# 16-wide attentions: contexts divided through DMA and VectorE instead of transposes, and one score unit moved behind the value products

## The chip, the cores and the metric

One core of a Trainium2 chip runs the whole program in one launch. The metric is the device time of one execution in microseconds. The kernel before took 1924.47 us (median of three runs, 1923.56 to 1924.92).

## The reference

Four layers on an input of 2 x 512 x 512 in float32; each is an attention and a feed-forward block, and both are followed by x = layernorm(x + block(x)). The attentions of layers 0, 2 and 3 have 32 heads of 16 values, and only these three are touched here. Layer 0 has 8 key and value heads, biases and rotary positions; layer 2 has 32 key and value heads and biases; layer 3 has 8 key and value heads, no biases and no rotation. In short:

```python
scores = einsum('bihd,bjhd->bhij', q, k) * SCALE      # d = 16
scores = where(causal, scores, lowest)
attn   = softmax(scores, axis=-1)
out    = einsum('bhij,bjhd->bihd', attn, v)           # heads joined again to 512 values: the context
return out @ wo
```

## The kernel before

The three 16-wide attentions are instances of one class, `Attention16`: a0 (layer 0, with rotation, here called narrow), a2 (layer 2, `wide`, 32 key heads) and a3 (layer 3, narrow, no rotation). Each runs 16 steps, one for a group of four heads: 8 groups for each of the two batches. Every engine has its own list of instructions, in program order; engines wait for one another on counting semaphores only.

A step `s` has ten slots `k` on TensorE (line 686 on). In slot k TensorE computes transposed scores of group s (`scoresT`, L574, into PSUM bank 4 or 5), ScalarE takes their exponential (`exp`, L1023) into the buffer PB, and GpSimd masks it (`causal`, L929). `scoresT` may only start when the exponential two slots earlier is done. So that the exponential stays in range, the maximum of every row is needed first: it comes from a first pass over the scores, two steps ahead. That pass is cut into six units a = 0 to 5 (`scores`, L539 and L541); VectorE takes the maximum of a unit straight after it (`maxima`, L801, L803, L806). Units use two pairs of PSUM banks in turn, so unit u waits until the maximum of unit u-2 is taken. GpSimd splits the maxima of a group into three bfloat16 parts (`split_max`, L913 to L919), TensorE transposes them in slot 3 of the next step (`max_T`, L551), ScalarE copies them (`take_max`, L1013), and the queue of SyncE (SP) writes them as three rows into KQ (`load_max`, L1107). Slot 0 of a step waits for that DMA.

Behind `max_T` in slot 3 stand the value products of the group before (`pv`, L595, 32 matmuls into bank 7). Their output lies transposed: 16 values and the sum of the probabilities for each head. ScalarE copies it to OT behind the exponential of slot 6 (`take_out`, L1040), TensorE turns it back in slot 8 (`back`, four transposes, L605), and VectorE divides by the sums (`norm`: a reciprocal at L815 and a product at L819) into CTX. In slot 1 of every odd step, two groups together are transposed again (`ctx_T`, L613), and ScalarE copies them to XTT (`take_ctx`, L1034), where the output projection reads them (`out_part`, L620).

Other work is spread over the steps. TensorE's part is in `aside`: the projections of the second batch (`project`, L485, and `project_v`, L500), and from step 10 (wide: 11) on the output projection of the first batch and the transposes of its layernorm (`turn_first`, L226). VectorE's part is in `beside(dve, st, s, a)`, called after the maximum of unit a: at a = 2 it does the rotation in a0 (`turn`, L765 to L768, in steps 2, 3, 5, 7, 9), the rounding rest in a3 (`take`, L752, same steps), `take_v` in a2 (L780, steps 1 and 2), and from step 11 (wide: 12) on the layernorm of the first batch (`mean`, L265 to L272, and one step later `finish`, L279). At k = 6 ScalarE's list has `middle` (L1004) in a3 ahead of `take_out`. GpSimd's list has `low` (L903) in a3 behind the mask of slot 8. In steps 2 to 5 and 10 to 13 of a0 and a2 it also has a bias addition (L979) behind slot 9.

SP's list in `sync` goes through groups: `load_max(G)` (done during step G-1), then `load_rows` of a late chunk (six to nine DMAs of the rounded parts into KQ: HI, MID, LOW), then, from G = 12, prefetches of weights. SP waits in this order, too.

These lines fix where the moved unit stands, and what VectorE does right behind it:

```python
if more and k in (0, 1, 2, 5, 6, 7):
    self.scores(pe, s + 2, (0, 1, 2, 5, 6, 7).index(k))
...
for a in range(6):
    if s + 2 < last:
        self.maxima(dve, s + 2, a)
    self.beside(dve, st, s, a)
```

Of the kernel before, what the change touches and what calls it, by code (L numbers as in the profile page):

```python
# [106 lines left out]
def build(nc, d, out):  # L107
# [11 lines left out]
    with ctx:  # L119
# [241 lines left out]
        def variances(dve, st, b):  # L361
# [10 lines left out]
        CTX = sb("CTX", [P, 2, NT, P], F32, A16)  # L372
# [9 lines left out]
        RC = sb("RC", [P, NT, 4], F32, A16)  # L382
        A16.close()
# [5 lines left out]
        AUX = 6  # L389
        s16 = {k: sig("a16_" + k) for k in (  # L390
            "ones_loaded proj_psum v_psum v_ready pads_ready turned rotated hi_ready rest_ready mid_ready lo_ready "
            "rows0_loaded rows1_loaded rows2_loaded scores_ready max_ready max_step max_parts maxT_psum maxT_ready "
            "max0_loaded max1_loaded scoresT_ready exp_ready probs_ready pv_ready outT_ready out_psum ctx_ready "
            "ctxT_psum ctxT_ready biased").split()}

        class Attention16(Stage):
            def __init__(self, W, Wo, nkv, scale, loaded, cols=None, vbias=None, rope=False, bo=None,
# [26 lines left out]
                    outT_ready=16, out_psum=16, ctx_ready=16, ctxT_psum=8, ctxT_ready=8,  # L424
# [175 lines left out]
            def back(self, pe, G):  # L600
# [56 lines left out]
            def tensor(self, pe):  # L657
# [29 lines left out]
                for s in range(last):  # L687
                    more = s + 2 < last
                    for k in range(10):
                        self.scoresT(pe, s, k)  # L690
                        self.aside(pe, s, k)
                        if more and k in (0, 1, 2, 5, 6, 7):
                            self.scores(pe, s + 2, (0, 1, 2, 5, 6, 7).index(k))
                        if k == 1 and s >= 3 and s % 2:
                            self.ctx_T(pe, (s - 3) // 2, 7)
# [5 lines left out]
                        if k == 8 and s:  # L701
                            self.back(pe, s - 1)
# [107 lines left out]
            def norm(self, dve, st, G):  # L810

                on = self.on
                dve.wait_ge(on["out_psum"].sem, on["out_psum"].at(G + 1))
                o = PS[:, 7, :].rearrange("p (t h e) -> p t h e", t=NT, h=4)
                st.link(dve.reciprocal(RC[:, :, :], o[:, :, :, HD]))  # L815
                if G >= 4 and G % 2 == 0:
                    dve.wait_ge(on["ctxT_psum"].sem, on["ctxT_psum"].at(G // 2 - 1))
                c = CTX[:, G // 2 % 2, :, G % 2 * 64:G % 2 * 64 + 64].rearrange("p t (h e) -> p t h e", e=HD)
                dve.tensor_tensor(c, o[:, :, :, 0:HD], RC[:, :, :].unsqueeze(3).to_broadcast([P, NT, 4, HD]),  # L819
                                  ALU.mult).then_inc(s16["ctx_ready"].sem, 1)  # L820

            def vector(self, dve, st):
# [30 lines left out]
                for s in range(last):  # L853
# [4 lines left out]
                    if s:  # L858
# [167 lines left out]
            def take_ctx(self, act, C, bank):  # L1026
# [3 lines left out]
                act.wait_ge(on["ctxT_psum"].sem, on["ctxT_psum"].at(C + 1))  # L1030
                if c == 0:
                    act.wait_ge(on["proj_psum"].sem, on["proj_psum"].at(self.each * (b + 1)))
                    act.wait_ge(on["v_psum"].sem, on["v_psum"].at((b + 1) * (NT if self.wide else 1)))
                act.copy(XTT[:, b, c, :], PS[:, bank, :]).then_inc(s16["ctxT_ready"].sem, 1)  # L1034

            def take_out(self, act, G):

                on = self.on
                act.wait_ge(on["pv_ready"].sem, on["pv_ready"].at(3 * G + 3))
                act.copy(OT[:, :], PS[:, 7, :]).then_inc(s16["outT_ready"].sem, 1)  # L1040

            def scalar(self, act):
# [59 lines left out]
            def load_max(self, sp, G):  # L1102
# [5 lines left out]
                  .then_inc(s16["max%d_loaded" % (G % 2)].sem, 16)  # L1108

# [35 lines left out]
            def sync(self, sp, prefetch):  # L1145
# [12 lines left out]
                for G in range(1, NB * GROUPS):  # L1158
                    self.load_max(sp, G)
# [1707 lines left out]
```

## Time and profile before

| | |
|---|---|
| median of three runs | 1924.47 us |
| profiled execution | 1924.28 us, its span 1922.6 us |
| mean granted TensorE clock | 0.993 of full speed |
| TensorE, VectorE, ScalarE, GpSimd busy | 95, 59, 45, 45% of the span |
| a0, 16 steps | from about 52 to 234 us of the span |
| a2, 16 steps | from about 1333 to 1529 us |
| a3, 16 steps | from about 1632 to 1810 us |

A profile lists instructions with start and length by engine. PE is TensorE's matmuls, PEld its weight loads, DVE VectorE, ACT ScalarE, POOL GpSimd, SPq the DMA issues of SyncE. An arrow in square brackets tells how long the engine stood still and whose work ended the wait. The length of a matmul includes its way through the array, so it is longer than the distance to the next one.

### The profile page before, as it was taken

The numbers are of one execution on the slowest core, as the hardware profiler recorded it, in microseconds if no ns is written. First come the engines' busy times: TensorE is split into PE (matmuls) and PEld (weight loads), VectorE is DVE, ScalarE is ACT, GpSimd is POOL, SyncE is SP. The second block draws the span as 40 slices with busy tenths as digits, with TensorE's granted clock in tenths as the row PEclk, the third lists the DMA queues.
The fourth block names the chain that finished last, engine by engine and source line by source line (L and its number), as shares of the span: only waits on it lengthen the run. The fifth ranks groups of instructions, "written<-read, shape, count | busy, mean of one in ns | idle before, by whom it ended". The sixth has DMA issues, their size and how long they took to land.

```text
span 1922.6 us, 29645 instructions
## 1 busy us (share of the span) xinstructions
PE 1828.2 (95%) x10760; PEld 1287.9 (67%) x10760; DVE 1130.6 (59%) x2433; ACT 859.2 (45%) x1896; POOL 871.5 (45%) x1383
## 2 busy tenths in 40 slices
PE   7999999999999999999999899999999999999998
PEld 3454447888888888888888687764455454555466
DVE  5677467666666666666666424235556355666465
ACT  1566544444444444444444433314466502565441
POOL 2465426555555555555554444323355312444352
PEclk9899999999999999999999999999999999999999
DMA  7213000101010101010100234205123104211101
GB/s 230 55 46 114 2 18 1 55 1 56 1 55 1 56 1 56 1 56 1 56 1 33 83 115 148 88 1 129 52 69 100 47 1 94 54 36 46 53 10 45
DMA packets 47201, 99.28 MB, mean 52 GB/s; under 512 B 8011, under 2 KB 36043, under 8 KB 43595
## 3 DMA queue, kind: packets, MB, share of 16 engines
q1 hardware_dynamic: 44464, 95.02, 15.6%
q10 hardware_dynamic: 2592, 2.36, 0.5%
q8 instruction: 87, 1.43, 0.3%
q14 instruction: 58, 0.48, 0.1%
HBM read 66.36 MB, written 2.10 MB: 36 GB/s over the span
## 4 chain that ended last, share of the span: by engine, by line
PE 76%; DVE 12%; ACT 4%; issue 3%; DMA 1%; POOL 1%; ACTq 1%; PEld 0%; SPq 0%; PEldq 0%; POOLq 0%; DVEq 0%
PE PS L1483 10%; PE PS L1582 9%; PE PS L485 6%; PE PS L2005 5%; PE PS L595 5%; PE PS L574 4%; PE PS L620 4%; PE PS L1560 4%; PE PS L1544 3%; DVE NM L801 3%; PE PS L2018 3%; PE PS L539 3%; PE PS L1512 3%; PE PS L1976 2%; PE PS L500 2%
## 5 line engine op out<-in xcount | busy, mean ns | idle before, releaser
L1023 ACT ACTIVATE PB<-PS 128x512 f32<-128x512 f32 x480 | 276.4, 600 | 213.1 <-PE PS L574 210.3
L929 POOL TENSOR_SCALAR_AFFINE_SELECT PB<-PB 128x256 f32<-128x256 f32 (+1 forms) x480 | 173.7, 369 | 283.6 <-ACT PB L1023 274.6
L801 DVE TENSOR_REDUCE NM<-PS 128x2 f32<-128x1024 f32 x192 | 206.8, 1090 | 147.3 <-PE PS L541 143.8
L574 PE MATMUL PS<-KQ 99*128 99x512 bf16 (+3 forms) x768 | 179.1, 305 | 9.3 <-ACT PB L1023 4.6
L1774 ACT CAST OTH<-PS 128x512 fp32r<-128x512 f32 x64 | 37.6, 587 | 309.5 <-PE PS L1565 309.5
L1901 POOL TENSOR_SCALAR PR<-PR,RCP 128x512 f32<-128x512 f32 (+3 forms) x256 | 135.5, 540 | 83.3 <-DVE RCP L1704 83.3
L1836 ACT ACTIVATE PR<-PR,NX 128x512 f32<-128x512 f32 (+3 forms) x256 | 145.0, 566 | 32.5 <-DVE NX L1698 29.3
L485 PE MATMUL PS<-XTT,WA 128*128 128x512 f32 x288 | 145.9, 613 | 13.5 <-DVE ident_masks_b L2647 12.0
L1698 DVE CUSTOM_DVE_ANT_0 PR<-PS,CAUSAL 128x512 f32<-128x512 f32 (+3 forms) x256 | 124.3, 486 | 53.3 <-PE PS L1531 52.0
L539 PE MATMUL PS<-KQ 99*128 99x128 bf16 (+2 forms) x576 | 125.2, 278 | 22.6 <-DVE NM L801 20.5
L1662 DVE TENSOR_TENSOR PTL<-PS,PTH 128x384 fp32r<-128x384 f32 (+2 forms) x256 | 115.5, 452 | 28.3 <-ACT PTH L1767 25.9
L541 PE MATMUL PS<-KQ 125*128 125x128 bf16 x768 | 126.9, 222 | 1.7 <-DVE NM L803 1.7
L295 POOL TENSOR_TENSOR rstd<-ve,halfneg 128x1 f32<-128x1 f32 x64 | 44.1, 689 | 168.9 <-DVE ve L272 168.9
L1544 PE MATMUL PS<-ident_masks,PR 128*128 128x128 f32 x640 | 111.9, 273 | 8.1 <-DVE PTL L1662 7.9
L574 PEld LDWEIGHTS PS<-KQ 99*128 99x128 bf16 x768 | 62.4, 99 | 78.4 <-issue 39.2
L539 PEld LDWEIGHTS PS<-KQ 99*128 99x128 bf16 x576 | 56.6, 99 | 78.2 <-DVE NM L801 43.7
L1690 DVE TENSOR_TENSOR XBB<-PS,XBB 128x512 f32<-128x512 f32 x64 | 44.3, 692 | 105.2 <-PE PS L1582 104.4
L1767 ACT CAST PTH<-PS 128x384 fp32r<-128x384 f32 (+2 forms) x256 | 101.0, 395 | 8.3 <-PE PS L1544 7.9
L1582 PE MATMUL PS<-Wo1H,OTL 128*128 128x512 f32 x256 | 102.1, 399 | 0.0
L1582 PE MATMUL PS<-Wo1H,OTH 128*128 128x512 f32 x256 | 100.9, 394 | 0.5 <-DVE OTL L1683 0.5
L1582 PE MATMUL PS<-Wo1L,OTH 128*128 128x512 f32 x256 | 100.4, 392 | 0.0
L541 PEld LDWEIGHTS PS<-KQ 125*128 125x128 bf16 x768 | 71.7, 99 | 39.2 <-issue 27.9
(333 smaller groups left out, 4578.4 us busy)
## 6 DMA issues: line engine op xcount, KB each, us to landing
KQ<-HI SPq DMA_DIRECT2D x90, 128.0 KB
KQ<-MID SPq DMA_DIRECT2D x72, 128.0 KB
WB<-f_w SPq DMA_DIRECT2D x12, 768.0 KB, 4.4
WB<-w1o SPq DMA_DIRECT2D x8, 1024.0 KB, 7.9
WC<-f_w SPq DMA_DIRECT2D x10, 768.0 KB, 4.4
WB<-w1a SPq DMA_DIRECT2D x8, 768.0 KB, 4.3
WB<-w1b SPq DMA_DIRECT2D x8, 768.0 KB, 5.8
WA<-w SPq DMA_DIRECT2D x6, 1024.0 KB, 6.4
```

The lines of the kernel that those rows point to most:

```text
L485: x = pe.matmul(PS[:, self.bank(m), :], self.W[:, c, at:at + P], XTT[:, b, c, :], start=(c == 0), stop=(c == NC - 1))
L539: pe.matmul(ps[:, 0:n - P], KQ[0:PR16, self.query(G, h), i * P:(i + 1) * P], KQ[0:PR16, self.key(G, h), 0:n - P], start=True, stop=True)
L541: x = pe.matmul(ps[:, n - P:n], KQ[0:KR, self.query(G, h), i * P:(i + 1) * P], KQ[0:KR, self.key(G, h), n - P:n], start=True, stop=True)
L574: x = pe.matmul(ps[:, at:at + T - j * P], KQ[0:PR16, self.key(s, h), j * P:(j + 1) * P], KQ[0:PR16, self.query(s, h), j * P:T], start=True ...
L801: x = dve.tensor_reduce(nm[:, h:h + 2, i], PS[:, b:b + 2, 0:(i + 1) * P], AX.X, ALU.max, negate=True)
L929: pool.affine_select(blocks, blocks, [[0, count], [1, P]], ALU.is_ge, 0.0, base=0, channel_multiplier=-1).then_inc(s16["probs_ready"].sem, 1)
L1023: act.activation(PB[:, n % PBS, :], PS[:, 4 + n % 2, :], ACT.Exp, scale=self.scale)\
L1483: x = pe.matmul(PS[:, p % 2, :], a[:, c, n:n + P], x[:, c, :], start=(c == 0 and i == 0), stop=(c == NC - 1 and i == 2))
L1544: x = pe.transpose(PS[:, 4 + i % 2, j * P:(j + 1) * P], PR[:, n % 2, OFF[t] + j * P:OFF[t] + (j + 1) * P], ident[:, :])
L1582: x = pe.matmul(PS[:, 6 + t % 2, :], o[:, h, t * P:(t + 1) * P], w[:, h, :], start=(h == 0 and i == 0), stop=(h == GQ - 1 and i == 2))
L1836: act.activation(PR[:, n % 2, at:at + w], PR[:, n % 2, at:at + w], ACT.Exp, scale=-1.0, bias=NX[:, n % 2, i:i + 1], accum_out=SM[:, n % 2, ...
L1901: pool.tensor_scalar(pr, pr, RCP[:, n % 2, i:i + 1], 1.0, ALU.mult, ALU.mult)\
```

## The change

The contexts of groups 0 to 13 no longer go back through TensorE. When OT is written, SP copies the sums of four heads to a tile SUMS spread over 128 partitions, and the 16 undivided rows of each head straight into XTT (`spread`, five DMAs for each group). For every two groups VectorE takes the reciprocal of SUMS (`invert`, behind the maximum of unit 1 in odd steps), SP brings it back into eight rows and from there repeats it over 128 partitions (`gather_inverse`, two DMAs, and `spread_inverse`, one), and in the next even step VectorE multiplies XTT by it in place (`scale_ctx`). The last two groups go the old way. ScalarE's copy in slot 1 goes, and the third score unit stands in slot 4, behind `pv`, instead of slot 2.

```diff
+        TURNED = NB * GROUPS - 2
...
                 elif part == 0:
-                    pe.wait_ge(on["ctx_ready"].sem, on["ctx_ready"].at(G))
-                    if G % 2 == 0:
-                        pe.wait_ge(on["ctxT_ready"].sem, on["ctxT_ready"].at(G // 2))
+                    pe.wait_ge(on["outT_ready"].sem, on["outT_ready"].at(G))
+                    if G > TURNED:
+                        pe.wait_ge(on["normed"].sem, on["normed"].at(TURNED // 2 + G - TURNED))
...
-                        if more and k in (0, 1, 2, 5, 6, 7):
-                            self.scores(pe, s + 2, (0, 1, 2, 5, 6, 7).index(k))
-                        if k == 1 and s >= 3 and s % 2:
-                            self.ctx_T(pe, (s - 3) // 2, 7)
+                        if more and k in (0, 1, 4, 5, 6, 7):
+                            self.scores(pe, s + 2, (0, 1, 4, 5, 6, 7).index(k))
...
-                        if k == 8 and s:
+                        if k == 8 and s > TURNED:
                             self.back(pe, s - 1)
...
+            def invert(self, dve, C):
+                on = self.on
+                dve.wait_ge(on["out_loaded"].sem, on["out_loaded"].at(160 * (C + 1)))
+                dve.reciprocal(SUMS[:, :, :], SUMS[:, :, :]).then_inc(s16["normed"].sem, 1)
+
+            def scale_ctx(self, dve, C):
+                on = self.on
+                b, c = divmod(C, NC)
+                dve.wait_ge(on["inv_loaded"].sem, on["inv_loaded"].at(48 * (C + 1)))
+                dve.tensor_tensor(XTT[:, b, c, :], XTT[:, b, c, :], SPREAD[:, :], ALU.mult)\
+                   .then_inc(s16["ctxT_ready"].sem, 1)
...
-                    if s:
+                    if s > TURNED:
                         self.norm(dve, st, s - 1)
...
+                if a == 1 and s >= 3 and s % 2:
+                    self.invert(dve, (s - 3) // 2)
+                if a == 1 and s >= 4 and s % 2 == 0:
+                    self.scale_ctx(dve, (s - 4) // 2)
+                if a == 5 and s == NB * GROUPS - 1:
+                    self.scale_ctx(dve, TURNED // 2 - 1)
...
                 act.wait_ge(on["pv_ready"].sem, on["pv_ready"].at(3 * G + 3))
+                if 1 <= G <= TURNED:
+                    act.wait_ge(on["out_loaded"].sem, on["out_loaded"].at(80 * G))
...
                         self.exp(act, s, k)
-                        if k == 1 and s >= 3 and s % 2:
-                            self.take_ctx(act, (s - 3) // 2, 7)
...
+            def spread(self, sp, G):
+                on = self.on
+                C, e = divmod(G, 2)
+                b, c = divmod(C, NC)
+                if c == 0 and e == 0:
+                    sp.wait_ge(on["proj_psum"].sem, on["proj_psum"].at(self.each * (b + 1)))
+                    sp.wait_ge(on["v_psum"].sem, on["v_psum"].at((b + 1) * (NT if self.wide else 1)))
+                sp.wait_ge(on["outT_ready"].sem, on["outT_ready"].at(G + 1))
+                loaded = s16["out_loaded"]
+                sp.dma_start(SUMS[:, e, :], OT[HD:P:32, :]).then_inc(loaded.sem, 16)
+                for h in range(4):
+                    a = 64 * e + HD * h
+                    sp.dma_start(XTT[a:a + HD, b, c, :], OT[32 * h:32 * h + HD, :]).then_inc(loaded.sem, 16)
+
+            def gather_inverse(self, sp, C):
+                on = self.on
+                sp.wait_ge(on["normed"].sem, on["normed"].at(C + 1))
+                if C:
+                    sp.wait_ge(on["inv_loaded"].sem, on["inv_loaded"].at(48 * C))
+                for e in range(2):
+                    sp.dma_start(INV[4 * e:4 * e + 4, :], SUMS[:, e, :]).then_inc(s16["inv_loaded"].sem, 16)
+
+            def spread_inverse(self, sp, C):
+                on = self.on
+                sp.wait_ge(on["inv_loaded"].sem, on["inv_loaded"].at(48 * C + 32))
+                if C:
+                    sp.wait_ge(on["ctxT_ready"].sem, on["ctxT_ready"].at(C))
+                sp.dma_start(SPREAD[:, :], INV[:, :].unsqueeze(1).to_broadcast([8, HD, T]))\
+                  .then_inc(s16["inv_loaded"].sem, 16)
...
-                for G in range(1, NB * GROUPS):
-                    self.load_max(sp, G)
+                for G in range(1, NB * GROUPS + 1):
+                    if G >= 4 and G % 2 == 0:
+                        self.gather_inverse(sp, (G - 4) // 2)
+                    if G < NB * GROUPS:
+                        self.load_max(sp, G)
+                    if G >= 4 and G % 2 == 0:
+                        self.spread_inverse(sp, (G - 4) // 2)
+                    if 2 <= G <= TURNED + 1:
+                        self.spread(sp, G - 2)
+                    if G == NB * GROUPS:
+                        break
                     if self.wide and G in (2, 3):
                         self.load_rows(sp, 4 + G)
                     if G - self.lag in self.late:
```

## Rows read from the trace of the kernel before

**Rows 1.** Page: busy time by engine; the chain that ended last, by engine.

```profile
PE 1828.2 (95%) x10760; PEld 1287.9 (67%) x10760; DVE 1130.6 (59%) x2433; ACT 859.2 (45%) x1896; POOL 871.5 (45%) x1383
...
PE 76%; DVE 12%; ACT 4%; issue 3%; DMA 1%; POOL 1%; ACTq 1%; PEld 0%; SPq 0%; PEldq 0%; POOLq 0%; DVEq 0%
```

**Rows 2.** Timeline of PE, a2, step 6: start, length, engine, line, operation.

```profile
1420.82 0.66 PE L605 MATMUL PS<-ident_masks,OT 128*128 128x128 f32 x4
1421.32 0.88 PE L574 MATMUL PS<-KQ 99*128 99x256 bf16 x3
```

**Rows 3.** Timeline, a0, steps 7 to 8.

```profile
137.31 2.36 PE L595 MATMUL PS<-PB,WC 128*32 128x512 f32 x32
...
138.28 0.74 DVE L765 SCALAR_TENSOR_TENSOR WB<-PS,bcols,WB 128x512 f32<-128x512 f32 x1
...
139.60 0.61 PE L574 MATMUL PS<-KQ 99*128 99x384 bf16 x4
...
140.59 1.82 DVE L801 TENSOR_REDUCE NM<-PS 128x2 f32<-128x768 f32 x2
...
143.46 0.33 PE L539 MATMUL PS<-KQ 99*128 99x384 bf16 x1
...
144.17 1.23 DVE L801 TENSOR_REDUCE NM<-PS 128x2 f32<-128x1024 f32 x1
...
145.46 0.34 PE L539 MATMUL PS<-KQ 99*128 99x384 bf16 x1 [0.73 <-DVE NM L801]
...
148.57 0.61 PE L574 MATMUL PS<-KQ 99*128 99x384 bf16 x4
```

**Rows 4.** Groups by line over the whole span: count, busy us, mean ns, idle before.

```profile
L1023 ACT ACTIVATE PB<-PS 128x512 f32<-128x512 f32 x480 | 276.4, 600 | 213.1 <-PE PS L574 210.3
...
L750 DVE TENSOR_TENSOR REST<-WB,HI 128x512 f32<-128x512 f32 x10 | 8.8, 875 | 1.7 <-POOL WB L896 1.3 <-issue 0.2 <-ACT HI L993 0.2
```

**Rows 5.** Timeline, a3, step 5 into step 6.

```profile
1692.54 0.68 DVE L752 TENSOR_TENSOR REST<-PS,HI 128x512 f32<-128x512 f32 x1
...
1698.39 1.16 POOL L903 TENSOR_TENSOR LOW<-REST,MID 128x512 bf16<-128x512 f32 x1
...
1700.97 0.23 PE L551 MATMUL PS<-ident_masks_b,NM 128*128 128x128 bf16 x1
```

**Rows 6.** Timeline, a0, step 12.

```profile
192.84 0.54 DVE L279 TENSOR_SCALAR XBB<-S,mv,rstd 128x512 f32<-128x512 f32 x1
...
194.16 0.61 PE L574 MATMUL PS<-KQ 99*128 99x384 bf16 x4
...
195.16 0.66 PE L226 MATMUL PS<-ident_masks,XBB 128*128 128x128 f32 x4 [0.39 <-DVE ve L272]
```

**Rows 7.** Timeline of SP's queue, a2, steps 9 and 10.

```profile
1458.14 1.88 SPq L1143 DMA_DIRECT2D KQ<-HI  x3
1460.42 1.19 SPq L1129 DMA_DIRECT2D KQ<-MID  x2
1462.71 0.55 SPq L1132 DMA_DIRECT2D KQ<-LOW  x1
1463.32 0.74 SPq L1107 DMA_DIRECT2D KQ<-NMT  x1
```

**Rows 8.** Timeline of PE, a2: first matmul behind the value products of steps 10 and 11.

```profile
1465.22 0.39 PE L574 MATMUL PS<-KQ 99*128 99x384 bf16 x2
...
1475.79 0.39 PE L574 MATMUL PS<-KQ 99*128 99x384 bf16 x2
```

**Rows 9.** Page, DMA issues: count, KB each, us from issue to landing.

```profile
out<-XBB SPq DMA_DIRECT2D x8, 256.0 KB, 2.4
```

**Rows 10.** Timeline of PE in a2, step 0.

```profile
1333.97 0.60 PE L574 MATMUL PS<-KQ 99*128 99x512 bf16 x1 [1.92 <-ACT PB L1023]
```

**Rows 11.** Busy time by engine in stretches, a2, steps 0 and 1; PEclk is the granted clock.

```profile
1330.59:1334.01 3.42, 1.50 (x10) 0.73 (x9) 2.49 (x4) 2.59 (x4) 2.01 (x6) 1.00 0.61 152
1334.01:1337.42 3.41, 3.41 (x9) 1.65 (x10) 0.26 (x1) 0.99 (x2) 0.86 (x3) 0.50 0.76 211
```

More of the change, by code:

```diff
@@ L371, in build @@
         PB = sb("PB", [P, PBS, T], F32, A16)
-        CTX = sb("CTX", [P, 2, NT, P], F32, A16)
+        CTX = sb("CTX", [P, NT, P], F32, A16)
         OT = sb("OT", [P, T], F32, A16)
@@ L382, in build @@
         RC = sb("RC", [P, NT, 4], F32, A16)
+        SUMS = sb("SUMS", [P, 2, 16], F32, A16)
+        INV = sb("INV", [8, T], F32, A16)
+        SPREAD = sb("SPREAD", [P, T], F32, A16)
         A16.close()
@@ L392, in build @@
             "rows0_loaded rows1_loaded rows2_loaded scores_ready max_ready max_step max_parts maxT_psum maxT_ready "
-            "max0_loaded max1_loaded scoresT_ready exp_ready probs_ready pv_ready outT_ready out_psum ctx_ready "
-            "ctxT_psum ctxT_ready biased").split()}
+            "max0_loaded max1_loaded scoresT_ready exp_ready probs_ready pv_ready outT_ready turned_psum normed "
+            "ctxT_ready biased out_loaded inv_loaded").split()}
         class Attention16(Stage):
@@ L423, in __init__ @@
                     max0_loaded=128, max1_loaded=128, scoresT_ready=160, exp_ready=160, probs_ready=160, pv_ready=48,
-                    outT_ready=16, out_psum=16, ctx_ready=16, ctxT_psum=8, ctxT_ready=8,
+                    outT_ready=16, turned_psum=3, normed=TURNED // 2 + 2, ctxT_ready=8,
+                    out_loaded=80 * TURNED, inv_loaded=24 * TURNED,
                     biased=NB * NT if bo is not None else 0)
@@ L812, in norm @@
                 on = self.on
-                dve.wait_ge(on["out_psum"].sem, on["out_psum"].at(G + 1))
+                dve.wait_ge(on["turned_psum"].sem, on["turned_psum"].at(G + 1 - TURNED))
                 o = PS[:, 7, :].rearrange("p (t h e) -> p t h e", t=NT, h=4)
                 st.link(dve.reciprocal(RC[:, :, :], o[:, :, :, HD]))
-                if G >= 4 and G % 2 == 0:
-                    dve.wait_ge(on["ctxT_psum"].sem, on["ctxT_psum"].at(G // 2 - 1))
-                c = CTX[:, G // 2 % 2, :, G % 2 * 64:G % 2 * 64 + 64].rearrange("p t (h e) -> p t h e", e=HD)
+                c = CTX[:, :, G % 2 * 64:G % 2 * 64 + 64].rearrange("p t (h e) -> p t h e", e=HD)
                 dve.tensor_tensor(c, o[:, :, :, 0:HD], RC[:, :, :].unsqueeze(3).to_broadcast([P, NT, 4, HD]),
-                                  ALU.mult).then_inc(s16["ctx_ready"].sem, 1)
+                                  ALU.mult).then_inc(s16["normed"].sem, 1)
+            def invert(self, dve, C):
[8 more added lines that the diff above has]
+                   .then_inc(s16["ctxT_ready"].sem, 1)
             def vector(self, dve, st):
@@ L1029, in take_ctx @@
                 b, c = divmod(C, NC)
[L1030 to L1033, printed above, removed]
+                act.wait_ge(on["turned_psum"].sem, on["turned_psum"].at(3))
                 act.copy(XTT[:, b, c, :], PS[:, bank, :]).then_inc(s16["ctxT_ready"].sem, 1)
@@ L1039, in take_out @@
                 act.wait_ge(on["pv_ready"].sem, on["pv_ready"].at(3 * G + 3))
+                if 1 <= G <= TURNED:
+                    act.wait_ge(on["out_loaded"].sem, on["out_loaded"].at(80 * G))
+                elif G > TURNED:
+                    act.wait_ge(on["turned_psum"].sem, on["turned_psum"].at(G - TURNED))
                 act.copy(OT[:, :], PS[:, 7, :]).then_inc(s16["outT_ready"].sem, 1)
```

8 lines of the change are left out of this document (4 added, 4 removed).

## Prediction

> **What bounds the kernel now.** I read the page first: PE is busy 95% of the span and makes up 76% of the chain that ended last, DVE 12% [rows 1]. A busy PE here is an average, so I went on to the timelines of the three attentions, step by step, and measured from the end of one step's value products to the end of the next's (P to P; I number such an interval by the step it begins in). The reader is to see three kinds. In a2 TensorE waits little, and the four transposes of `back` cost it 0.50 us each time (1420.82 to 1421.32) [rows 2]. In a0's intervals without a projection (5, 7, 9) VectorE is the bound: it goes without a gap from the rotation (138.28) into the maxima of units 3 and 4 (140.59) and on; the interval is 139.60 to 148.57, 8.97 us [rows 3]. And in most intervals PE waits for the maximum of unit 0 before unit 2 (0.73 us at 145.46) [rows 3]. What matters most: while the value products run (137.31 to 139.60, 2.3 us [rows 3]), VectorE is at work in the intervals that have much for it. The maximum of unit 2 comes before them, and so the work called behind it at a = 2 is done under them: the rotation begins at 138.28 and ends at 140.55, P is 139.60 [rows 3]; `finish` and `mean` begin at 192.84, P is 194.16, and PE's `turn_first`, which needs them, waits only 0.39 us [rows 6].
>
> **The change, part by part.** All differences are against the profiled execution (1924.28 us; its span 1922.6 and 1.7 outside), which is 0.2 us below the median of the runs.
>
> *Removed from PE.* `back` 0.50 us in 14 steps of each attention, `ctx_T` (four transposes of the same kind, taken at 0.45) in 7: 10 us per attention, 30 in all. This is worth something only where PE ends the interval. The wait for the maximum of unit 0 goes as well: unit 2 comes so late that it is long done. In an interval with a projection (PE has over 3 us more work there, so nothing else is late) the gain is 0.50 + 0.73 = 1.2 us [rows 2, 3]; with `ctx_T` in it, the wait is shorter by as much, and the sum the same. There are 3 in a0 (1, 6, 8) and 6 in a3 (1 to 4, 6, 8): -11. In a0's interval 4 GpSimd's bias addition and split come next: -0.3. First intervals of the output projection: a0 and a3 -0.9, a2 -0.5, together -2.3. The last two steps have no score units and gain both transposes: -1.0 each, -3.0. Gains: -16.4 us.
>
> *Moved: unit 2.* Now its scores follow `scoresT` of slot 4, 0.2 us behind P. A unit's maximum starts 0.71 us behind its first matmul (143.46 to 144.17) and lasts 1.23, less a little overlap [rows 3]: it stands from P+0.9 to P+2.1, and everything called at a = 2 starts only then. VectorE idles under the value products instead.
>
> - a0, intervals 5, 7, 9: rotation 2.3 us (138.28 to 140.55) to P+4.4; maximum of unit 3, 0.9 (half of the 1.82 pair), to 5.3 [rows 3]; unit 5 uses the same banks, so PE issues it at 5.35. Slot 8 follows, its exponential of 0.6 [rows 4] starts at 6.25; two more hand-overs of `scoresT` and exponential lead to slot 0 at 6.9, and slot 3's `scoresT` to 8.9; GpSimd's split, held by the masks, ends at 9.0; `max_T` and value products (0.15 + 2.3): 11.4 against 8.97, +2.4 each, +7.3. Intervals 2 and 3 have a projection that covers part: +1.1 and +0.6.
> - a3, intervals 5, 7, 9: `take` 0.68 [rows 5] ends at 2.8 instead of before P; ScalarE's list has MID (0.6) and the copy to OT (0.6) behind it and ahead of slot 7, so the exponentials of slots 7 and 8 come 1.0 later. Before, `max_T` was already waiting for what comes behind (`low` 1.16 from 1698.39, mask, split; 1700.97) [rows 5]. +1.0 each, +3.0.
> - a2, intervals 1 and 2: `take_v` (0.7) comes later in the same way, +0.8 each, +1.6. Intervals 3 to 9: unit 2's 0.44 us now delays `scoresT` of slot 5, then two exponentials, the copies and slot 0: what `back` and `ctx_T` free is used up, 0. At best 0.50 + 0.22 are gained in each of 7 (-5), at worst unit 2's 0.44 is lost (+3); I take 0.
> - Intervals with `mean` alone (11 in a0 and a3, 12 in a2): +0.8 each, +2.4.
> - Intervals 12 and 13 of a0 and a3, 13 of a2: `finish` and `mean` take 2.26 us (192.84 to 195.10); they now begin at P+2.1 and end at 4.3, `turn_first` starts at 4.4 instead of 1.0 (195.16 - 194.16) [rows 6]: 3.4 us later, less `back`, `ctx_T`, the wait and unit 2 itself, +2.1 and +2.5: +11.7.
>
> *Added to VectorE.* `invert` and `scale_ctx` stand at a = 1, in the idle time under the value products, which is longer than 2 us. Neither is in the trace: `scale_ctx` is bounded by 0.4 and the 0.88 us of a product that reads two tiles of SBUF [rows 4], `invert` by 0 and the same. I take 0 on the path. They take the place of `norm` (0.7 us in every step). If the cover were gone, 0.9 in each of 14 steps, +12.
>
> *Added to SP.* Five DMAs a group, three more for two groups, 0.55 to 0.75 us of issue each (taken as 0.6) [rows 7]: 3 to 5 us a step, beside at most 5 for `load_rows`; steps last 9 to 12. Landing is taken as 2.4 us [rows 9], though the small pieces of SUMS could take less or twice that. `load_max` then still lands ahead of slot 0, with one exception. `spread(8)` waits until the last projection of the second batch is done. In a0 and a3 it is, in a2 the last chunk is projected in slots 1 to 4 of step 10, while `spread(8)` stands in step 9's part of the queue. Behind it wait `load_rows` of chunk 14 (1.88 + 1.19 + 0.55 = 3.62) and `load_max(11)`, which before was issued at 1463.32, 1.9 us ahead of P [rows 7]. After: 1.35 (projection done) + 3.0 + 3.6, with gaps P+8.1, landed at 10.5; slot 0 of step 11 would want it at 5.5. From slot 0 to the next P it is 4.5 us: 15.0 against 10.6 before (1465.22 to 1475.79) [rows 8], +4.4. With 0.3 us for each of the five it is +2.9, with a landing of 4.5 it is +6.5; a gain is excluded by SP's order.
>
> Losses: 7.3 + 1.7 + 3.0 + 1.6 + 2.4 + 11.7 + 4.4 = 32.1. Schedule: 32.1 - 16.4 = +15.7.
>
> *Clock.* In a2's step 0 PE stood still for 1.92 us up to 1333.97 [rows 10]; from 1334.01 on the granted clock is 0.50, 1.2 GHz instead of 2.4, for 3.4 us [rows 11]. The change makes six stretches where PE stands still for 3.4 us or more: before `turn_first` in five intervals, and before slot 0 of a2's step 11. Each should bring such a fall. It costs at most half of 3.4 us, where all of PE's work in it is on the path; I take 1.0, +6 in all (0 to +10).
> The Trainium skill (TensorE: Matmul & The Clock Gate, section "Why this matters for your kernels") has a rule against this: leave no long idle gap between bursts of matmuls, or the clock drops back to half. By that rule the six falls come and the time is that of the sum; without it the sum would end 6 us lower. The trace agrees so far as one such stretch goes [rows 10, 11].
>
> Forecast: 1924.3 + 15.7 + 6 = 1946 us.
>
> **Rivals.** *PE is the bound after all.* If the maxima behind P do not hold the chain (work at a = 2 finds room), the 30 us of transposes come back wherever PE is on the path, and 0.73 more in the narrow steps: 16.4 us from the intervals counted above, and about 8 from a2's, whose PE waits little: 1924 - 24 = 1900. For it: 95% [rows 1]. Against it: VectorE's list has the a = 2 work behind unit 2, and [rows 3, 6] show it finishing only just in time now. It decides if PE's next need of VectorE lies later than P+4.4. *Gains and losses cancel:* the five `turn_first` intervals (11.7) or the SP stall turn out half as long and the clock stays: 1924 to 1930. *Schedule without falls:* 1940. *SP is the bound in all of a2:* if an issue takes 0.75 and DMAs of 64-byte pieces land in 4.5 us, `load_max` misses slot 0 in some seven further steps by 1.5 us: 1946 + 10 = 1956 or more.
>
> **How the numbers follow.** Forecast (1946, its own range 1940 to 1953) 0.45; schedule without falls 0.18; SP bound 0.15; cancelling 0.10; PE the bound 0.12. Range: 1918 to 1960, which leaves out most of the PE case and the far end of SP's. A measurement of this kernel can tell about 0.2% (3.8 us) from no change. Faster has the PE case and a little of the cancelling one: 0.13; within 0.2%: 0.07; slower: 0.80.
>
> **What would show it.** Right: in a0's interval 7 DVE idles under the value products, L765 starts over 2 us behind P, and PE waits for DVE before unit 5; in a0's step 12 PE L226 starts 4 us behind P after a wait for DVE; in a2 one long wait of PE, some 4 to 5 us, before slot 0 of step 11, with L1107 issued some 8 us behind P; granted clock 0.5 in these places. Intervals with a projection in a0 and a3 are 1.2 us shorter. Wrong: a rotation still done by P+1, `turn_first` without a wait, or a shorter a2.

## The result and the profile after

The changed kernel takes 1998.37 us (median of 4 runs, 1995.15 to 2001.27), the kernel before 1924.01 (4 runs on the same chip): ratio 1.0397, 95% interval 1.0384 to 1.0409. Slower was forecast, at 1946 us within 1918 to 1960; the loss is 74 us instead of 22. The profiled execution spans 1996.8 us with a mean granted clock of 0.972; before, 1922.6 us and 0.993. One run of E4 below took 4621 us, far above the others, and is left out of its median.

The page, busy time and the chain that ended last, to be held against [rows 1]:

```profile
PE 1834.5 (92%) x10508; PEld 1276.6 (64%) x10508; DVE 1122.2 (56%) x2391; ACT 852.6 (43%) x1875; POOL 875.4 (44%) x1383
...
PE 74%; DVE 13%; issue 4%; ACT 3%; POOL 1%; DMA 1%; SPq 1%; ACTq 1%; PEld 0%; PEldq 0%; POOLq 0%; DVEq 0%
```

PE issues 252 instructions fewer and is busy for longer: part of its work ran at half clock. The page can't say where. I measured all intervals of both timelines from P to P as in the prediction, and put them in the prediction's groups (us against before, sums over the group; E1 to E3 are the first three experiments below). Interval 15 ends where PE's next instruction behind the last value products starts:

| intervals | predicted | changed | E1 | E2 | E3 |
|---|---|---|---|---|---|
| projection: a0 and a3 1, 6, 8 | -7.2 | -7.3 | -1.8 | -3.4 | -3.7 |
| projection: a3 2 to 4 | -3.6 | +0.4 | -1.1 | +2.3 | -2.1 |
| rotation with projection: a0 2, 3 | +1.7 | +7.7 | -1.0 | +7.0 | -1.4 |
| rotation: a0 5, 7, 9 | +7.3 | +13.4 | -0.4 | +14.4 | +0.4 |
| `take`: a3 5, 7, 9 | +3.0 | +3.1 | +1.4 | +3.1 | +2.9 |
| a2 1 to 9 | +1.6 | +3.4 | +0.3 | +6.0 | +0.2 |
| `mean` alone | +2.4 | +5.4 | -1.3 | +3.7 | -1.5 |
| `finish`, `mean`, `turn_first` | +11.7 | +24.3 | +3.5 | +26.2 | +1.9 |
| a2 10 (SP) | +4.4 | +6.8 | +7.7 | +0.7 | +6.8 |
| first output projection, a0 4 | -2.6 | -1.1 | -0.6 | +1.3 | -0.7 |
| the last two, 14 and 15 | -3.0 | +21.1 | +20.0 | 0.0 | +20.8 |

Predicted come 6 us for the clock on top; measured, the clock is inside the rows. The changed column sums to 77; the span outside these intervals is 2.8 us shorter.

**a0, interval 7**, timeline of PE and DVE (start, length; in brackets idle time and what ended it); it answers to [rows 3]:

```profile
146.39 0.39 PE L579 MATMUL PS<-KQ 99*128 99x384 bf16 x2
147.26 1.23 DVE L804 TENSOR_REDUCE NM<-PS 128x2 f32<-128x1024 f32 x1 [2.27 <-PE PS L546]
148.40 0.74 DVE L768 SCALAR_TENSOR_TENSOR WB<-PS,bcols,WB 128x512 f32<-128x512 f32 x1
151.72 0.23 PE L544 MATMUL PS<-KQ 99*128 99x128 bf16 x1 [2.44 <-DVE NM L804]
```

P is 146.39. The maximum of unit 2 runs from P+0.87, the rotation starts at P+2.01, unit 5 at P+5.33 (5.35 was predicted). Up to there the schedule is the predicted one. What follows shows in the view of windows (from:to, length, busy time of PE, PEld, DVE, ACT, POOL, granted clock, DMA share, GB/s):

```profile
146.39:151.86 5.47, 2.48 (x27) 1.61 (x24) 4.54 (x6) 2.83 (x5) 1.92 (x3) 1.00 0.34 62
151.86:158.69 6.83, 6.57 (x33) 2.87 (x35) 5.00 (x6) 3.90 (x8) 4.29 (x13) 0.50 0.34 47
158.69:160.10 1.41, 1.41 (x28) 0.58 (x21) 0.00 (x0) 0.00 (x0) 0.00 (x0) 1.00 0.04 9
```

For 6.83 us TensorE gets the lower of its two clocks, 1.2 instead of 2.4 GHz, and in that stretch PE is busy nearly all the time: units, `scoresT` and value products are on the path at half speed. The interval is 13.71 us; predicted was 11.4. In all, the records show 113 us at half clock in 22 stretches, 31 us in five before. Of the 113 us, 88 lie in the 45 intervals, where the kernel before has none.

**a0, step 12**, `finish` on DVE and `turn_first` on PE, against [rows 6]:

```profile
210.67 0.54 DVE L279 TENSOR_SCALAR XBB<-S,mv,rstd 128x512 f32<-128x512 f32 x1
...
212.99 0.86 PE L226 MATMUL PS<-ident_masks,XBB 128*128 128x128 f32 x4 [3.28 <-DVE ve L272]
```

P is 208.65, so `turn_first` starts at P+4.34 (predicted P+4.4) after a wait of 3.28 us instead of 0.39. Half clock follows from 213.30.

**a2, interval 10**: `spread(8)` and `load_max(11)` on SP's queue, and PE's slot 0 of step 11; it answers to [rows 7, 8]:

```profile
1499.00 0.56 SPq L1140 DMA_DIRECT2D SUMS<-OT  x1
...
1506.08 0.79 SPq L1127 DMA_DIRECT2D KQ<-NMT  x1
1508.52 0.59 PE L579 MATMUL PS<-KQ 99*128 99x512 bf16 x1 [3.21 <-DMA KQ<-NMT]
```

P is 1497.66: issued at P+1.34 and P+8.42 (predicted 1.35 and 8.1), slot 0 starts at P+10.9 (10.5 was predicted for the landing). The chain is as predicted; half clock lies over it for 10.2 us from 1503.54.

**Interval 15, which the prediction had at a gain.** a0, DVE and PE:

```profile
249.85 0.35 DVE L827 RECIPROCAL SUMS<-SUMS 128x32 f32<-128x32 f32 x1 [10.72 <-DMA XTT<-OT]
...
260.01 0.69 DVE L834 TENSOR_TENSOR XTT<-XTT,SPREAD 128x512 f32<-128x512 f32 x1 [9.45 <-DMA SPREAD<-INV]
260.62 0.25 DVE L818 RECIPROCAL RC<-PS 128x16 f32<-128x16 f32 x1
...
261.43 3.86 PE L600 MATMUL PS<-PB,WC 128*32 128x512 f32 x32 [5.03 <-issue]
```

The last value products, `pv(15)`, wait for `norm(14)`, and on VectorE that stands behind `scale_ctx` of the seventh context (a = 5 of step 15), which waits for two DMAs in a row. PE stands for 5.03 us, and the value products then take 3.86 us, mostly at half clock, instead of 2.36 [rows 3]. In a3 the same wait is longer; SP and DVE:

```profile
1863.13 0.42 SPq L2663 DMA_DIRECT2D WA<-f_b  x1
1864.22 1.28 SPq L1152 DMA_DIRECT2D INV<-SUMS  x2
1872.04 0.68 SPq L1160 DMA_DIRECT2D SPREAD<-INV  x1
1879.07 0.69 DVE L834 TENSOR_TENSOR XTT<-XTT,SPREAD 128x512 f32<-128x512 f32 x1 [14.52 <-DMA SPREAD<-INV]
```

SPREAD<-INV, which waits for INV<-SUMS, is issued 7.8 us after it (2.7 us in a0, 250.23 to 252.96): ahead of both stands the 1152 KB prefetch f_b, landed 8.8 us after its issue, at 1871.9. SPREAD<-INV itself takes 7.03 us more.

### The profile page after: what moved, and what is told of

Read it like the earlier page. It is cut to its first block, busy times and chain, and to the rows that moved or that the text cites. A ratio compares the mean times of both kernels' runs of the same rounds, so it can differ in the third digit from the quotient of the medians.

```text
span 1996.8 us, 29411 instructions
## 1 busy us (share of the span) xinstructions
PE 1834.5 (92%) x10508; PEld 1276.6 (64%) x10508; DVE 1122.2 (56%) x2391; ACT 852.6 (43%) x1875; POOL 875.4 (44%) x1383
## 3 DMA queue, kind: packets, MB, share of 16 engines
q10 hardware_dynamic: 2592, 2.36, 0.5%
## 4 chain that ended last, share of the span: by engine, by line
PE 74%; DVE 13%; issue 4%; ACT 3%; POOL 1%; DMA 1%; SPq 1%; ACTq 1%; PEld 0%; PEldq 0%; POOLq 0%; DVEq 0%
PE PS L1545 9%; PE PS L1644 9%; PE PS L600 6%; PE PS L490 5%; PE PS L2067 5%; PE PS L579 4%; PE PS L625 4%; PE PS L1622 3%; PE PS L1606 3%; PE PS L2080 3%; DVE NM L804 3%; PE PS L1574 3%; PE PS L544 3%; PE PS L2038 2%; PE PS L505 2%
## 5 line engine op out<-in xcount | busy, mean ns | idle before, releaser
L950 POOL TENSOR_SCALAR_AFFINE_SELECT PB<-PB 128x256 f32<-128x256 f32 (+1 forms) x480 | 178.2, 379 | 301.8 <-ACT PB L1044 294.3
L579 PE MATMUL PS<-KQ 99*128 99x512 bf16 (+3 forms) x768 | 189.2, 315 | 21.0 <-ACT PB L1044 17.0
L544 PE MATMUL PS<-KQ 99*128 99x128 bf16 (+2 forms) x576 | 130.9, 288 | 28.7 <-DVE NM L804 24.9
L546 PE MATMUL PS<-KQ 125*128 125x128 bf16 x768 | 132.6, 229 | 1.7 <-DVE NM L806 1.7
L579 PEld LDWEIGHTS PS<-KQ 99*128 99x128 bf16 x768 | 65.2, 101 | 106.3 <-issue 53.2
L544 PEld LDWEIGHTS PS<-KQ 99*128 99x128 bf16 x576 | 58.7, 103 | 84.7 <-DVE NM L804 50.9
L625 PE MATMUL PS<-WA,XTT 128*128 128x512 f32 x192 | 103.3, 640 | 3.0 <-DVE ve L272 3.0
```

The lines of the kernel that those rows point to most:

```text
L544: pe.matmul(ps[:, 0:n - P], KQ[0:PR16, self.query(G, h), i * P:(i + 1) * P], KQ[0:PR16, self.key(G, h), 0:n - P], start=True, stop=True)
L546: x = pe.matmul(ps[:, n - P:n], KQ[0:KR, self.query(G, h), i * P:(i + 1) * P], KQ[0:KR, self.key(G, h), n - P:n], start=True, stop=True)
L579: x = pe.matmul(ps[:, at:at + T - j * P], KQ[0:PR16, self.key(s, h), j * P:(j + 1) * P], KQ[0:PR16, self.query(s, h), j * P:T], start=True ...
L625: return pe.matmul(PS[:, bank, :], XTT[:, b, c, t * P:(t + 1) * P], self.Wo[:, c, :], start=(c == 0), stop=(c == NC - 1))
L950: pool.affine_select(blocks, blocks, [[0, count], [1, P]], ALU.is_ge, 0.0, base=0, channel_multiplier=-1).then_inc(s16["probs_ready"].sem, 1)
```

## Experiments

Theory: the moved unit uncovers VectorE's work behind it, the pauses bring half-clock stretches that are themselves on the path, and the DMA path costs only where a list waits for a landing. Rivals: the DMA path costs in every step; or the clock plays no part.

**E1, the unit back in slot 2**

```diff
-                        if more and k in (0, 1, 4, 5, 6, 7):
+                        if more and k in (0, 1, 2, 5, 6, 7):
```

> The changed kernel with the third score unit back in slot 2; the contexts still go through DMA. My theory (the moved unit exposes VectorE's work behind it, and the pauses bring half-clock stretches; the DMA path costs only at two places): the intervals of rotation, take and mean (a0 2, 3, 5, 7, 9, 11 to 13; a2 12, 13; a3 5, 7, 9, 11 to 13), which lost 54 us together, come back to the kernel before's, their half-clock stretches go, and interval 15 of the three attentions (+22.6) and a2's interval 10 (+6.8) stay lost: about 1950 us (1942 to 1962). Rival (the DMA path and its waits are the main cost): at most 15 us come back, over 1980.

Measured: 1948.89 us, ratio to before 1.0143 (1.0116 to 1.017). Of the 54 us nearly all come back, interval 15 and a2's interval 10 stay. The +3.5 in the row of `finish` is one new loss, 4.4 in a0's interval 12 (see E3). The sum for a2 hides another: its interval 8 loses 2.5, and PE waits 1.6 us for `load_max` there.

**E2, the kernel before with the unit alone moved**

```diff
-                        if more and k in (0, 1, 2, 5, 6, 7):
+                        if more and k in (0, 1, 4, 5, 6, 7):
```

> The kernel before with only the third score unit moved to slot 4; contexts still divided after transposes. My theory: the same intervals of rotation, take and mean lose about what they lost in the change (54 us), interval 15 and a2's interval 10 lose nothing: about 1975 us (1962 to 1985), and half-clock stretches in these intervals. Rival (the DMA path is the main cost, the moved unit a small one): under 1945.

Measured: 1978.88 us, 1.0303 (1.0273 to 1.0334). The two halves of the change nearly add up: 3.0% for the unit (E2) and 1.4% for the division (E1), against 4.0% together. In a0's interval 9 PE waits before unit 5 for 2.44 us, as in the changed kernel's interval 7. Half clock sets in at 176.50, within that wait, with no DMA in the division at all:

```profile
177.14 0.29 PE L539 MATMUL PS<-KQ 99*128 99x128 bf16 x1 [2.44 <-DVE NM L801]
```

The windows view of that stretch:

```profile
176.50:183.30 6.80, 6.16 (x33) 3.91 (x37) 5.39 (x8) 3.36 (x7) 3.79 (x12) 0.50 0.00 0
```

**E3, the unit stays in slot 4, VectorE's work goes ahead of it**

```diff
-                if a == 2 and ...   # take_v, turn or take, finish, mean
+                if a == 1 and ...   # the same, ahead of invert and scale_ctx
```

> The changed kernel, and VectorE's work of a = 2 (rotation, take, take_v, finish, mean) called at a = 1, ahead of the moved unit's maximum and so under the value products. My theory: the losses of these intervals go although the unit stays in slot 4, the gains of 1.2 in the intervals with a projection stay, the losses of interval 15 (+22.6) and of a2's interval 10 (+6.8) stay: about 1945 us (1935 to 1957), without half-clock stretches in the rotation intervals. Rival (the pauses come from unit 2 itself, which uses the banks later, whatever VectorE does): under 15 us come back, over 1983.

Measured: 1942.41 us, 1.0112 (1.0084 to 1.014). So it is not the unit that costs, but what stands behind it. a0, interval 7, DVE's rotation and PE's value products at both ends:

```profile
130.78 2.36 PE L600 MATMUL PS<-PB,WC 128*32 128x512 f32 x32
131.34 0.74 DVE L768 SCALAR_TENSOR_TENSOR WB<-PS,bcols,WB 128x512 f32<-128x512 f32 x1
...
139.77 2.36 PE L600 MATMUL PS<-PB,WC 128*32 128x512 f32 x32
```

The rotation is under the value products again, and the interval is 8.99 us. What E1 and E3 show anew, in a0's interval 12, is a prefetch that comes late; SP, then PE:

```profile
180.41 0.56 SPq L1140 DMA_DIRECT2D SUMS<-OT  x1
181.01 6.34 SPq L1143 DMA_DIRECT2D XTT<-OT  x4
187.40 0.58 SPq L2644 DMA_DIRECT2D WC<-f_w  x1
...
189.86 0.83 SPq L1127 DMA_DIRECT2D KQ<-NMT  x1
...
199.61 0.48 PE L579 MATMUL PS<-KQ 99*128 99x512 bf16 x1 [3.97 <-DMA KQ<-NMT]
```

`spread` stands ahead of a0's prefetches (3.7 MB) in the list, and one of its issues takes long, so they go out late. `load_max(13)`, queued behind them at 189.86, is there only some 9.7 us after its issue, and PE waits 3.97 us for it.

**E4, `scale_ctx` of the seventh context behind `norm(14)`**

```diff
-                if a == 5 and s == NB * GROUPS - 1:      # in beside
-                    self.scale_ctx(dve, TURNED // 2 - 1)
+                self.scale_ctx(dve, TURNED // 2 - 1)     # behind the loop over the steps
```

> The changed kernel, with VectorE's scale_ctx of the seventh context behind the norm of group 14 instead of ahead of it. My theory: pv(15) no longer waits for the DMA round trip (sums to INV, INV to SPREAD), only the output projection behind it does: interval 15 gains 4.5 in a0, 3.8 in a2, 5 in a3, about 13 us: 1985 (1981 to 1990). Rival (the interval is late by back(14) at half clock, not by the order on VectorE): under 4 us, over 1994.

Measured: 1986.58 us (median of three runs), 1.0332 (1.0294 to 1.0369). Interval 15 gains 4.7 in a0, 3.9 in a2 and 4.7 in a3. a0, PE:

```profile
255.12 2.36 PE L600 MATMUL PS<-PB,WC 128*32 128x512 f32 x32
259.34 1.13 PE L625 MATMUL PS<-WA,XTT 128*128 128x512 f32 x2 [1.85 <-DVE XTT L834]
```

The value products no longer wait and run at full clock; the output projection behind them waits for the rest.

**E7 and E8, the clock by itself**: in the changed kernel, one or two of the three instructions of a0's rotation are called at a = 1.

```diff
+                if self.rope and a == 1 and s - 1 in self.late:
+                    self.turn(dve, self.late[s - 1], 0)          # the first one (E7) or two (E8)
...
-                    self.turn(dve, self.late[s - 1]) if self.rope else ...
+                    self.turn(dve, self.late[s - 1], 1) if self.rope else ...   # the rest
```

> The changed kernel; in a0 one of the three instructions of the rotation is called at a = 1, under the value products, two stay behind the moved unit's maximum. a0's intervals 5, 7, 9 lost 4.5 each, of which I had put 2.4 on the schedule and nothing on the clock. My theory (the rest is half clock, brought by the pause of TensorE): the interval loses at least the 0.75 of one instruction, and more only if the half-clock stretch gets shorter or goes. Rival (the schedule was too small, the clock plays no part): 0.75 exactly, to +3.7, whatever the clock does.

> The same with two of the three instructions early. My theory: the pause of TensorE is 1.5 us shorter and the half-clock stretch goes, so that a0's intervals 5, 7, 9 fall to +1 or less: 3.5 us for 1.5 us of VectorE's work. Rival (clock plays no part): +3.0. If the half-clock stretch stays at its length, the interval decides nothing.

Measured (one execution each): 1993.54 and 1989.59 us. a0's intervals 7 and 9 lose 4.75 and 4.45 with none early, 3.78 and 3.91 with one, 0.69 and 0.68 with two. These lines show PE's wait before unit 5 of interval 7 on the timeline, and a stretch of the interval in the windows view, for E7:

```profile
147.12 0.29 PE L544 MATMUL PS<-KQ 99*128 99x128 bf16 x1 [1.68 <-DVE NM L811]
```

```profile
146.77:153.60 6.83, 6.22 (x33) 3.13 (x37) 5.14 (x7) 3.90 (x8) 4.40 (x13) 0.50 0.43 56
```

The same for E8, where the window is the whole interval:

```profile
143.86 0.23 PE L544 MATMUL PS<-KQ 99*128 99x128 bf16 x1 [0.79 <-DVE NM L811]
```

```profile
140.20:149.86 9.66, 7.61 (x82) 4.20 (x79) 6.70 (x8) 6.72 (x13) 5.53 (x15) 1.00 0.40 61
```

From E7 to E8 VectorE's work shrinks by 0.75 us, the intervals by 3.1 and 3.2: the half-clock stretch is gone, and was worth 2.4 us. (From none to one they gave 1.0 and 0.5, the stretch staying; so E7 by itself fits the rival's +3.7 too, and E8 decides.) The rival's +3.0 is out for intervals 7 and 9. Interval 5 missed its +1: it kept a half-clock stretch of 3.4 us in E8, and with it +3.0. An estimate for the schedule alone: these two intervals lose 0.0 with all three instructions early (E3) and 0.7 with two, both without half clock, so they would lose some 2 with none, near the 2.4 predicted; the rest of the 4.75 and 4.45 is the clock.

The other runs allow the same comparison where only `mean` is late. E4 changes nothing in a3's interval 11, and PE waits there for the same 0.54 and 0.99 us as in the changed kernel. The windows view of that interval, in the changed kernel and then in E4:

```profile
1806.57:1820.96 14.39, 12.61 (x89) 6.20 (x86) 8.23 (x11) 6.43 (x12) 5.26 (x15) 0.88 0.37 75
```

```profile
1799.83:1812.56 12.73, 10.95 (x89) 5.50 (x86) 8.18 (x11) 6.43 (x12) 5.24 (x15) 1.00 0.42 84
```

The instructions are the same. The first has a half-clock stretch of 3.41 us from 1810.74, the second none, and the difference is 1.66 us. Without it the interval loses 0.7 against the kernel before (predicted 0.8), with it 2.35. So the clock has a price here too. The length of a pause does not settle by itself whether a fall comes: the same waits came with one and without.

**E5 and E6, the waits taken out**, from E3 and from E1: E4's edit, and SP's list in another order.

```diff
+                    if self.wide and G == 11:
+                        self.spread(sp, 8)                   # behind load_max(11)
-                    if 2 <= G <= TURNED + 1:
+                    if 2 <= G <= TURNED + 1 and not (self.wide and G == 10):
                         self.spread(sp, G - 2)
+                    if G >= 13:
+                        prefetch(sp, G - 13)                 # was G - 12, at the end
```

> The changed kernel with VectorE's work of a = 2 called at a = 1, scale_ctx of the seventh context behind norm of group 14, and SP's list in another order: in a2 spread(8) stands behind load_max(11), and every prefetch of weights stands one step later, behind load_max and spread. My theory (three waits on SP's list and one order on VectorE are all that is left of the loss): against the run with only the early work (1942), a2's interval 10 gains 6.8, a0's interval 12 gains 4.5, interval 15 gains 18 (a0 to +2, a2 to 0, a3 to +2.5): 1913 us (1907 to 1922), faster than the kernel before. Rival (DMA landings are long, and the late prefetches or spread(8) only stall the next step): over 1930.

> The same order of SP's list and the same place of scale_ctx, with the third score unit in slot 2 and VectorE's work at a = 2 as in the kernel before: the division through DMA alone, its waits taken out. My theory: against the run with the unit back (1949) about 30 us go (interval 15: 18; a2 interval 10: 7.5; a0 interval 12: 4.9): 1919 us (1912 to 1927). The rival that the DMA path costs in every step, through SP or ScalarE, has it over 1930.

Measured: 1922.38 us, 1.001 (1.0 to 1.002), and 1932.56 us, 1.0051 (1.0034 to 1.0067). Both miss their expectation, by 9 and 14 us. Interval 15 comes down to +4.7 in all in E5, as expected, but a2's interval 10 gains only 1.6 (ScalarE's copy to OT now waits 2.2 us for `spread(8)`), and a0's interval 14 now loses 2.9 in E5 and 5.7 in E6. By E5's SP queue the prefetches, a step later, now hold back INV<-SUMS (issued at 200.46, followed by SPREAD<-INV only at 206.63), `spread` goes out late behind it, and ScalarE's copy to OT waits 1.75 us for that. The rival has a share: part of each wait moved on.

**E9 to E11, other orders of the DMAs**, on E5 (E10: with the unit in slot 2 and the work at a = 2): two OT buffers, a0's prefetches one a step, `scale_ctx` at a = 4; in E9 and E10 `spread` stands ahead of `spread_inverse`, in E11 only in a0. E9 also has a2's unit in slot 2 from step 3 on. In all three, SP also waits for INV's landing ahead of both, and ahead of each `spread` for the landing of the one before.

```diff
-        OT = sb("OT", [P, T], F32, A16)
+        OT = sb("OT", [P, 2, T], F32, A16)
...
-                    if G >= 4 and G % 2 == 0:
-                        self.spread_inverse(sp, (G - 4) // 2)
                     if 2 <= G <= TURNED + 1 ...:
                         self.spread(sp, G - 2)
+                    if G >= 4 and G % 2 == 0:                # E11: here for a0, above for a2 and a3
+                        self.spread_inverse(sp, (G - 4) // 2)
```

> The kernel with the early work, and what was still late in it taken out: OT has two buffers (so ScalarE's copy no longer waits for spread of the group before), a0's loads of the next layers go out one a step behind spread instead of together, spread stands ahead of spread_inverse on SP's list, scale_ctx stands behind the maximum of unit 4, and from step 3 on a2's third score unit stands in slot 2, a0's and a3's in slot 4. My theory (the division through DMA costs nothing where no list waits for a landing): against that run (1922) a0's interval 14 gains 2.9, a2's interval 10 about 4 and its intervals 3 to 9 0.5 each, a0's and a3's even intervals about 1 each: 1908 us (1902 to 1917), faster than the kernel before by over 0.2%. Rival (SP's list is full, each DMA taken from one place is late at another): 1918 or more.

> The same order of the DMAs, with the third score unit in slot 2 in all three attentions and VectorE's work at a = 2 as in the kernel before: the division alone. My theory: 1914 us (1908 to 1921), faster than before by the transposes alone, and about 6 us behind the mixed one, which is what the unit in slot 4 is worth once VectorE's work stands ahead of it. Rival (SP's list is full): 1925 or more, no faster than the kernel before.

> The kernel with two OT buffers again, but in a2 and a3 spread_inverse stands ahead of spread, as in the change (only a0 keeps it behind), and a2's unit is in slot 4 again. What went wrong in the run before, by its trace, is that SPREAD<-INV fills the queue and whatever stands third behind it is issued some 4 us late: in a2 and a3 that was load_rows or a prefetch, with load_max behind them (a2 intervals 4, 6, 8, 12: +1.1 to +5.8; a3 6 and 8: +2.1, +2.2). My theory (it is this order, not the number of DMAs): these go, a0 stays at -5.5, a2 comes to -1, a3 to -6: 1911 us in the conditions of the run with the early work fixed (1922), 1903 to 1918, ratio to the kernel before under 0.998. Rival (SP's list is full, an order only moves the wait): 1922 or more.

Measured: E9 1935.87 us, 1.0069 (1.0048 to 1.0089); E10 1937.9, 1.0094 (1.0079 to 1.0109); E11 1919.21, 0.9986 (0.9974 to 0.9998). E9 and E10 are clear misses; E11 misses by 8 us, and its interval only just lies below the time before. (E9's profiled execution took 1927.2 us, among its shortest, so its intervals hold less than the loss of the median.) E9's a3, SP's queue:

```profile
1744.10 0.70 SPq L1162 DMA_DIRECT2D SPREAD<-INV  x1
1744.90 5.78 SPq L1198 DMA_DIRECT2D KQ<-HI  x3
```

Three issues that take 1.9 us together elsewhere [rows 7] take 5.78 behind SPREAD<-INV; `load_rows` and then `load_max` come late, and a3's intervals 6 and 8 lose 2.1 and 2.2. In E3's rows it was XTT<-OT (6.34 for four, 2.5 otherwise). So one cause may stand behind many of the small waits: this DMA is slow. E12 tests it.

**E12, the reciprocals on sixteen rows** (on E11)

```diff
-                    sp.dma_start(INV[4 * e:4 * e + 4, :], SUMS[:, e, :])...
+                    for i in range(2):                       # every row twice
+                        sp.dma_start(INV[8 * e + i:8 * e + 8:2, :], SUMS[:, e, :])...
...
-                sp.dma_start(SPREAD[:, :], INV[:, :].unsqueeze(1).to_broadcast([8, HD, T]))
+                sp.dma_start(SPREAD[:, :], INV[:, :].unsqueeze(1).to_broadcast([16, HD // 2, T]))
```

> The run by attention, and INV has sixteen rows instead of eight (each row twice, gathered by four DMAs instead of two), so that SPREAD<-INV repeats each row 8 times instead of 16. SPREAD<-INV took 7.1 us from issue to landing in every attention, and by its packets only 7 to 8 of the 16 DMA engines were at work on it. My theory (a DMA that reads 8 rows goes over 8 engines): with 16 rows it lands in 4.5 to 5 us, the DMA third behind it is issued without the 4 us, and interval 15 of a0 and a3 gains 1.5 to 2.5 although two more DMAs stand in the chain: some 5 us less than the run by attention (1919), 1914 (1909 to 1919), ratio to the kernel before 0.996. Rival (the landing goes with the 128 partitions written, or with the bytes): 7 us as before, and the two DMAs more cost 1.2 us in each chain: 1921.

Measured: 1908.64 us (1908.3 to 1910.65), 0.9938 (0.9925 to 0.9951): 0.6% faster than the kernel before. That is 5 us below the expectation and just outside its range, on the good side. A window inside the last SPREAD<-INV of a0, in the changed kernel and then in E12 (the last two columns are the DMA share and GB/s), and behind them what waits for it in E12 on the timeline:

```profile
254.50:259.00 4.50, 1.82 (x9) 0.83 (x8) 0.00 (x0) 1.68 (x4) 1.31 (x4) 1.00 0.47 50
```

```profile
224.10:226.30 2.20, 2.20 (x18) 0.55 (x20) 0.44 (x2) 0.59 (x1) 0.81 (x2) 1.00 0.93 101
```

```profile
227.22 0.69 DVE L834 TENSOR_TENSOR XTT<-XTT,SPREAD 128x512 f32<-128x512 f32 x1 [2.65 <-DMA SPREAD<-INV]
```

The share of busy DMA engines doubles, and the landing falls from 7.1 to 4.6 us (issued at 222.66). Interval 15 is at +1.6 in all, and the two groups of projection intervals are at -7.3 and -3.6, the predicted gains.

The rival's two more DMAs do cost something: a0's intervals 7 and 9 lose 2.4 and 1.2 in E12 and nothing in E11. E12's interval 7, SP, then PE:

```profile
132.54 2.35 SPq L1154 DMA_DIRECT2D INV<-SUMS  x4
134.94 0.77 SPq L1126 DMA_DIRECT2D KQ<-NMT  x1
...
137.33 0.38 PE L579 MATMUL PS<-KQ 99*128 99x512 bf16 x1 [1.64 <-DMA KQ<-NMT]
```

P is 131.59. The four issues of INV<-SUMS take 2.35 us, the two of E11 1.18, so `load_max(8)` goes out at P+3.35 instead of P+2.17, and PE waits 1.64 us for it before slot 0. Interval 9 has the same wait. In interval 7 half clock lies over 3.4 us behind it, in interval 9 none.

## Why the prediction was wrong

Right, by its own steps:

- The direction and the main mechanism: the work at a = 2 comes behind unit 2, and PE then waits for it. P+5.33 and P+4.34 in the traces, and E3, which only calls VectorE's work earlier, show it.
- The SP stall in a2's interval 10: the issue times are within 0.4 us, the landing of `load_max` took the 2.4 us (1506.08 to 1508.52), and E2 (without these DMAs) doesn't have the stall.
- The gain of 1.2 us in six of nine projection intervals; `take` in a3.

Wrong, in a size or in what lies on the path:

- **"It costs at most half of 3.4 us ... I take 1.0, +6 in all": this term failed.** I counted six falls, where PE stands still for 3.4 us or more. All six came, but four of them lasted 6.8 or 10.2 us. Falls also came where the longest pause was 2.44 us (rotation), 1.68 us (E7) or 0.99 us (a3's interval 11); the pause in my own [rows 10] was 1.92 us, and I counted only longer ones. The price per fall was too low as well: E7 and E8 give 2.4 us for one 6.83 us stretch, a3's interval 11 gives 1.66 for one of 3.41. If the five `turn_first` intervals cost as much beyond their predicted schedule (24.3 - 11.7 = 12.6, 2.5 each), a0's rotation (13.4 - 7.3, and 7.7 - 1.7) 12.1, `mean` alone 3.0 and a2's interval 10 2.4, that is 30 us where I had 6. For a0's intervals 7 and 9 and a3's interval 11 the runs show the clock as the cause; for the others it rests on their rows at 0.50 and on the matching schedule.
- **"The last two steps ... -3.0" and "I take 0 on the path" for `scale_ctx`: these steps failed**, by 24 us. The lengths were within my bounds (0.69 and 0.35 us in the rows), but I looked at the scaling in the middle steps, where it has a step's time, and not at the last one, which stands ahead of `norm(14)`, that PE needs. (Interval 14 did gain, 1.6 of the 3.0.) E4 shows the order on VectorE as the cause of 13.3 of the 22.7 us of interval 15; with f_b behind the chain (E5) a3 gains another 4.9, and the shorter landing (E11 to E12) takes 4.5 off the three.
- Landing "taken as 2.4 us" from [rows 9]: SPREAD<-INV takes 7.1. The row I took was of the store of the result, a transfer of another shape.
- a3's intervals 2 to 4, 4.0 us in all: I counted -1.2 each although `take` and `take_v` stand at a = 2 there, too. In E3 intervals 2 and 3 show the -1.2.

The rival of the SP-bound a2 was not met in the changed kernel (+0.1 to +0.5 in intervals 3 to 9), but E9 shows that it was near. The rival "PE is the bound after all" is what E12 comes to, at 1909 instead of 1900.

Left open: what decides whether a pause brings a fall of the clock.

## What to carry to other kernels

Before moving an item on an in-order list, write down what the other engines call right behind it: here the item cost nothing, and what it pushed out from under 2.3 us of matmuls cost 54 us. A pause of TensorE has a second price in the work that follows it at half clock; add it wherever that work is on the path. And look at the last turn of a pipelined chain by itself: what is hidden for six contexts was on the path for the seventh.

## What was not expected of the hardware

- A DMA that repeats 8 rows over 128 partitions (256 KB) ran at 50 GB/s with 0.47 of the DMA engines busy; from 16 rows it ran at 101 GB/s with 0.93. The Trainium skill (DMA: Bandwidth & Descriptors, section "Why a DMA increments its semaphore by 16 and not by 1") says that a transfer goes over the largest number of engines up to 16 that divides the leading dimension of both sides; 8 rows make 8. The two shares agree with it.
- While such a transfer was under way, the second DMA behind it took some 4 us to issue on the same queue (E3's four XTT<-OT: 6.34 us, 2.5 otherwise). With 16 rows four of them took 3.79 us.
- A small DMA behind large loads on the same queue landed only with them (SPREAD<-INV, which waits for INV<-SUMS, followed it by 7.8 us behind f_b and by 2.7 without).
- The granted clock fell to 0.50 behind a pause of PE of 2.44 us (changed kernel, a0's interval 7), within one of 1.68 us (E7), and behind one of 0.99 us (changed kernel, a3's interval 11). With the same 0.99 us it did not fall in E4, and with 0.79 us it did not fall in E8's interval 7. The Trainium skill (TensorE: Matmul & The Clock Gate, section "Why this matters for your kernels") warns of long idle gaps between bursts; its rule agrees in kind, but by its gap alone, as I read it for the prediction, these falls would not have come.
